# A pre-norm transformer block with ternary feed-forward weights on one core: the normalisation of attention in two halves, Q and K three slots ahead, row normalisation on VectorE, and Q and K columns of the first weight first

## The reference

```
h = layernorm(x)                          # rows of 512, no gain
qkv = h @ Wqkv                            # Wqkv: 512 x 1536, 16 heads of 32
a = softmax(causal(q @ k.T * 32**-0.5))   # a batch and a head: 512 x 512
x = x + (a @ v) @ Wo
y = layernorm(x)
w = clip(round(w / mean|w|), -1, 1) * mean|w|     # for w1, w3 (1365 x 512), w2 (512 x 1365)
x = x + (silu(y @ w1.T) * (y @ w3.T)) @ w2.T
```

## Time and profile before

| | |
|---|---|
| median of 3 runs | 706.42 us (706.09 to 708.06) |
| profiled execution | 708.65 us |
| its span, first to last instruction | 706.9 us |
| TensorE matmul busy | 596.1 us, 84% |
| VectorE busy | 368.9 us, 52% |
| GpSimd busy | 347.5 us, 49% |
| ScalarE busy | 254.2 us, 36% |
| mean granted TensorE clock | 0.939 |

### The profile page before, as it was taken

One profiled execution on the slowest core, in us unless ns is written; L12 is line 12 of the kernel. 1 busy time (PEld: TensorE's weight loads), 2 busy tenths in 40 slices (PEclk: granted clock), 3 DMA queues, 4 the chain that ended last, 5 costly groups with the idle time before them and its releaser, 6 DMA issues.

```text
span 706.9 us, 9375 instructions
## 1 busy us (share of the span) xinstructions
PE 596.1 (84%) x3392; PEld 278.4 (39%) x3392; DVE 368.9 (52%) x917; ACT 254.2 (36%) x428; POOL 347.5 (49%) x364
## 2 busy tenths in 40 slices
PE   1866767776699798999998879999998986899998
PEld 1323224333244344444444334444443432444443
DVE  7486646636554656462565656453646553353431
ACT  1563618526223244422223424322333363202330
POOL 6350569355438295625083784433472754652330
PEclk9989786978899989999999999999999997899999
DMA  9743223131401200222304000223020000100001
GB/s 339 230 139 116 76 75 121 45 100 46 135 1 56 80 1 1 75 77 74 120 2 134 1 1 23 85 88 128 24 65 11 2 1 1 60 31 30 1 1 59
DMA packets 35569, 46.87 MB, mean 66 GB/s; under 512 B 4634, under 2 KB 25114, under 8 KB 35524
## 3 DMA queue, kind: packets, MB, share of 16 engines
q1 hardware_dynamic: 35524, 46.28, 20.1%
HBM read 33.55 MB, written 12.58 MB: 65 GB/s over the span
## 4 chain that ended last, share of the span: by engine, by line
PE 50%; POOL 18%; DVE 14%; ACT 8%; issue 4%; DMA 3%; SPq 1%; DVEq 0%; POOLq 0%; ACTq 0%
PE work L971 29%; PE work L1133 9%; DVE o_sb L837 6%; POOL xn L525 4%; POOL early L563 4%; ACT early L660 4%; PE work L1081 4%; POOL early L566 3%; POOL early L554 3%; DVE masked L828 2%; PE score_bank L1042 2%; PE work L1095 2%; PE prob_bank L1064 2%; POOL early L569 2%; DMA late<-in_L_attn_Wqkv 2%
## 5 line engine op out<-in xcount | busy, mean ns | idle before, releaser
L971 PE MATMUL work<-late,w_ternary 128*128 128x512 f16 (+1 forms) x704 | 170.3, 393 | 5.2 <-DVE o_sb L842 3.0
L828 DVE CUSTOM_DVE_ANT_0 masked<-score_bank,mask 128x512 f16<-128x512 f32 (+3 forms) x256 | 111.7, 485 | 14.1 <-PE score_bank L1042 14.0
L660 ACT ACTIVATE early<-prob_bank,scalars 128x512 f32<-128x512 f32 x160 | 100.7, 686 | 39.1 <-PE prob_bank L1064 38.8
L971 PEld LDWEIGHTS work<-late,w_ternary 128*128 128x128 f16 (+1 forms) x704 | 71.5, 103 | 83.7 <-issue 10.7
L580 POOL TENSOR_TENSOR late<-late 128x512 f16<-128x512 f32 (+1 forms) x44 | 50.7, 1157 | 81.6 <-ACT late L680 81.6
L1064 PE MATMUL prob_bank<-q_stack,k_stack 98*128 98x512 f16 (+3 forms) x256 | 58.3, 328 | 29.1 <-ACT early L660 28.6
L837 DVE RECIPROCAL o_sb<-work 128x512 f32<-128x512 f32 x16 | 53.7, 3358 | 47.4 <-PE work L1095 47.4
L1133 PE MATMUL work<-w_ternary,late 128*128 128x512 f16 (+1 forms) x352 | 78.0, 379 | 0.0
L574 POOL TENSOR_TENSOR ot_lo<-o_sb,ot_hi 128x512 f16<-128x512 f32 x16 | 18.5, 1157 | 117.4 <-ACT ot_hi L665 117.4
L1042 PE MATMUL score_bank<-k_stack,q_stack 96*128 96x512 f16 (+3 forms) x256 | 55.4, 321 | 19.5 <-DVE row_max L828 15.7
L858 DVE SCALAR_TENSOR_TENSOR late<-late,work 128x512 f32<-128x512 f32 (+1 forms) x44 | 30.2, 687 | 78.9 <-ACT late L673 78.9
(11 more groups left out here) (114 smaller groups left out, 857.4 us busy)
## 6 DMA issues: line engine op xcount, KB each, us to landing
xn<-in_L_attn_x SPq DMA_DIRECT2D x16, 256.0 KB, 4.1
q_stack<-q_hi_spill SPq DMA_DIRECT2D x32, 128.0 KB, 2.5
k_stack<-k_hi_spill SPq DMA_DIRECT2D x32, 128.0 KB, 2.6
late<-in_L_attn_Wqkv SPq DMA_DIRECT2D x4, 768.0 KB, 8.7
x_res<-in_L_attn_x SPq DMA_DIRECT2D x12, 256.0 KB, 2.9
out_y<-x_res SPq DMA_DIRECT2D x12, 256.0 KB, 2.0
late<-in_L_ffn_w SPq DMA_DIRECT2D x4, 682.5 KB, 4.1
early<-in_L_ffn_w SPq DMA_DIRECT2D x3, 768.0 KB, 13.8
```

The lines of the kernel that those rows point to most:

```text
L660: act.activation(probs[:, u, :], prob_bank[u % 2][:], ACT.Exp, scale=scalar(exp_scale)).then_inc(prob_free, 1)
L828: dve.tensor_tensor_reduce(masked[:, k % 2, 0:n], score_bank[u % 2][:, off:off + n], mask[:, S - n:S], 1.0, LOWEST, ALU.add, ALU.max, row_ ...
L971: last = pe.matmul(bank, lhs, rhs, start=(n == 0), stop=(n == len(terms) - 1))
```

## The change

- `sums` no longer normalises. A new step `normalise` with two halves of 256 columns does it: the first behind the first `probs` piece, the second behind the scores that follow. Both work banks come free with the second half.
- A new step `ot` (ScalarE and GpSimd) stands ahead of piece 2 of `probs`.
- `q` and `k` of slot s+3 are made in slot s; their halves go to a place of their own in DRAM for each slot, and a step `stack` loads the stacks of s+2 at the head of slot s. The first four slots' Q and K are made before slot 0.
- `norm` moves from GpSimd to VectorE. The second norm writes to `yn`, a new buffer of two row blocks; `xn` holds x alone.
- The loads of Wqkv bring the columns of Q and K first (four loads of 512 KB) and V in one. Q and K, V, and Wo have maxima and scales of their own.
- wo's maximum and split move from the prelude to slot 0. The mean of w3 and w2 comes one step later, with all that follows it. x of batch 1 is normalised and turned in slot 0, of batch 2 normalised in slot 3 and turned in slot 4.
- The down products of batch b-2 are laid in slot 0 of batch b (before: in slot 3 of batch b-1, for batch b-2), the projections and both sets of transposes too; slots 1 to 3 hold 6, 8 and 8 of the up products.

```diff
 def preparation(m, start):
-    steps[start + PARTS] = [("weight_mean", m)]
+    steps[start + PARTS + 1] = [("weight_mean", m)]
...
-        a = start + PARTS + 1 + c // 2
+        a = start + PARTS + 2 + c // 2
...
 def slot(s, early, late):
-    front = [[("scores", s + 1, 0)], [("scores", s + 1, 1)]] if s + 1 < SLOTS else [[]]
-    o = spread(front, early)
-    if s:
-        o += [("values", s - 1), ("sums", s - 1)]
+    o = [("scores", s + 1, 0)] if s + 1 < SLOTS else []
+    o += sum((steps for _, steps in early), []) + ([("values", s - 1)] if s else [])
+    o += [("scores", s + 1, 1)] if s + 1 < SLOTS else []
+    o += [("sums", s - 1)] if s else []
     back = []
     for p in range(PIECES):
-        back.append([("probs", s, p)])
+        back.append([("ot", s - 1)] if s and p == 2 else [])
+        back[-1].append(("probs", s, p))
         if s + 1 < SLOTS and p + 2 < PIECES:
             back.append([("scores", s + 1, p + 2)])
+        if s and p == 0:
+            back = [[("probs", s, 0), ("normalise", s - 1, 0)] + (back[1] if s + 1 < SLOTS else []) + [("normalise", s - 1, 1)]]
...
+def residual_rows(b, i):
+    return (2.5, [("project", b, i), ("stats_y", b, i), ("norm_y", b, i)])
...
 def order():
...
+    o += [("top_part", c) for c in range(KC)] + [("xt", 0, 0), ("xt", 0, 1), ("top_turn", "qk"), ("xt", 0, 2)]
+    o += [("xt", 0, 3), ("top_spread", "qk"), ("x_load", 1)] + [("split", j) for j in range(4)] + [("top_v",), ("q", 0)]
+    o += [("weight_sum", w1, 0), ("k", 0), ("top_turn", "v"), ("stack", 0), ("q", 1), ("top_spread", "v")]
+    o += [("weight_sum", w1, 1), ("split", 8), ("k", 1), ("stack", 1), ("weight_sum", w1, 2)]
...
+    o += [("weight_ternary", w1, c) for c in range(6, 9)] + [("q", 3), ("max_row", 0)]
...
+    o += [("k", 3)] + [("weight_turn", w1, c) for c in range(8, HC)]
...
-        early, late = qk(s + 2) if g != GROUPS - 2 else [], []
+        early, late = [(0.0, [("stack", s + 2)])] if 0 < s < SLOTS - 2 else [], []
+        ahead = 0 < s < SLOTS - 3
+        if ahead:
+            early += [(2.5, [("q", s + 3)])]
         if b == 0:
             late = {p: prep.pop(PIECES * s + p, []) for p in range(PIECES)}
...
+            if ahead:
+                late[0].insert(0, ("k", s + 3))
+            if g == 0:
+                late[0] += [("stats_x", 1, 0), ("stats_x", 1, 1), ("wo_max",)]
+                late[1] += [("stats_x", 1, 2), ("stats_x", 1, 3), ("norm_x", 1, 0), ("norm_x", 1, 1)]
+                late[2] += [("norm_x", 1, 2), ("norm_x", 1, 3), ("top_turn", "wo"), ("xt", 1, 0)]
+                late[3] += [("top_spread", "wo"), ("xt", 1, 1), ("xt", 1, 2)]
+                late[4] += [("wo_split",), ("xt", 1, 3), ("x_load", 2)]
+            elif g == GROUPS - 1:
+                late[1] += [("res_load", 0, i) for i in range(ST)]
+                for i in range(ST):
+                    late[i] += [("stats_x", 2, i)]
+                    late[i + 1] += [("norm_x", 2, i)]
         elif g == 0:
...
+            late = [(4.7, [("down", b - 2, i), ("res_load", b - 1, i)]) for i in range(ST)] if b > 1 else []
+            late += v[:1] + [(1.0, steps) for _, steps in sorted(prep.items())]
+            late += v[1:3] + y[:2] + v[3:] + yt[:1] + y[2:3] + yt[1:2] + y[3:]
             prep = {}
+            if not last:
+                late += [(0.4, [("xt", b + 1, i)]) for i in range(ST)] + [(0.0, [("x_load", b + 2)])]
+            early_yt = yt[2:]
             ups = ffn_up(b - 1)
...
+            n = 8 if g > 1 else 6
+            late, ups = ups[:n], ups[n:]
+            if g == GROUPS - 1 and b + 2 < BATCHES:
+                late = merged(late, [(0.3, [(step, b + 2, i)]) for step in ("stats_x", "norm_x") for i in range(ST)])
+        if b and ahead:
+            late.insert(0, (2.5, [("k", s + 3)]))
...
+            def stack(s):
+                if s >= STACKS:
+                    sp.wait_ge(prob_full, NU * (s - STACKS + 1))
+                else:
+                    sp.wait_ge(unit_rows_set, s + 1)
+                for n, stacks in (("q", q_stack), ("k", k_stack)):
+                    for part_ in ("hi", "lo"):
+                        sp.wait_ge(spilled[n, part_], 16 * (s + 1))
+                        for j in [j for j, at in enumerate(STACK_ROWS[n]) if at == part_]:
+                            sp.dma_start(stacks[s % STACKS][j * HD:(j + 1) * HD, :, :],
+                                         spill[n, part_][s].rearrange("(h d) s -> d h s", h=HG)).then_inc(stacked[n][s % STACKS], 16)
...
+            def norm(n, b, src, dst, i):
+                dve.wait_ge(rstd_done[n], ST * b + i + 1)
+                dve.tensor_scalar(dst, src, mean_var[n][:, i, 0:1], rstd[n][:, i:i + 1],
+                                  ALU.subtract, ALU.mult).then_inc(norm_done[n], 1)
+
+            def norm_y(b, i):
+                if i > 1:
+                    full(dve, ("yt", b, i - 2))
+                elif b:
+                    full(dve, ("yt", b - 1, i + 2))
+                norm("y", b, residual(b, i), yn[:, i % 2, :], i)
...
+            def normalise(s, part_):
+                cols = slice(part_ * S // 2, (part_ + 1) * S // 2)
+                sums, values = ("sums", s), ("values", s)
+                if part_ == 0:
+                    full(dve, sums)
+                    full(dve, values)
+                    if s:
+                        dve.wait_ge(o_lo_done, s)
+                    dve.reciprocal(o_sb[:, cols], work[bank_of(sums)][:, cols]).then_inc(inverted, 1)
+                    dve.wait_ge(inverted, s + 1)
+                    dve.tensor_tensor(o_sb[:, cols], work[bank_of(values)][:, cols], o_sb[:, cols], ALU.mult)
+                else:
+                    dve.reciprocal(o_sb[:, cols], work[bank_of(sums)][:, cols]).then_inc(work_free[bank_of(sums)], 1)
+                    emptied(dve, sums)
+                    dve.tensor_tensor(o_sb[:, cols], work[bank_of(values)][:, cols], o_sb[:, cols],
+                                      ALU.mult).then_inc(work_free[bank_of(values)], 1)
```

More of the change, by code:

```diff
@@ L155, in order @@
     o = [("pad", w1)] + [("stats_x", 0, i) for i in range(ST)] + [("norm_x", 0, i) for i in range(ST)]
[L156 to L166, removed]
@@ new lines, in order @@
+    o += [("weight_sum", w1, 1), ("split", 8), ("k", 1), ("stack", 1), ("weight_sum", w1, 2)]
+    o += [("v", 0, 0), ("weight_sum", w1, 3), ("scores", 0, 0), ("split", 4), ("split", 5), ("v", 0, 1)]
+    o += [("weight_mean", w1), ("scores", 0, 1)] + [("weight_round", w1, c) for c in range(HC)]
+    o += [("q", 2), ("weight_ternary", w1, 0), ("scores", 0, 2), ("k", 2), ("stack", 2), ("split", 6), ("split", 7)]
+    o += [("weight_ternary", w1, 1), ("weight_ternary", w1, 2), ("pad", w3)]
+    o += [("weight_load", w3, j) for j in range(PARTS)] + [("scores", 0, 3), ("v", 0, 2)]
@@ L169, in order @@
+    o += [("weight_ternary", w1, c) for c in range(3, 6)] + [("weight_turn", w1, 0), ("weight_turn", w1, 1)]
+    o += [("scores", 0, 4), ("v", 0, 3)] + [("weight_turn", w1, c) for c in range(2, 5)]
+    o += [("weight_ternary", w1, c) for c in range(6, 9)] + [("q", 3), ("max_row", 0)]
+    o += [("weight_ternary", w1, c) for c in range(9, HC)] + [("weight_turn", w1, c) for c in range(5, 8)]
+    o += [("k", 3)] + [("weight_turn", w1, c) for c in range(8, HC)]
     prep = preparation(w3, 0)
@@ L291, in build @@
         k_stack = [sb(f"k_stack{i}", [P, HG, S], F16) for i in range(STACKS)]
-        spill = {key: nc.dram_tensor("_".join(key) + "_spill", [P, S], F16, kind="Internal").ap() for key in half}
+        spill = {key: nc.dram_tensor("_".join(key) + "_spill", [SLOTS, P, S], F16, kind="Internal").ap() for key in half}
         masked = sb("masked", [P, 2, S], F16)
@@ L361, in build @@
         res_loaded = [sem(f"res_loaded{i}") for i in range(ST)]
-        wqkv_loaded = [sem(f"wqkv_loaded{i}") for i in range(KC)]
+        qk_loaded = [sem(f"qk_loaded{i}") for i in range(KC)]
+        v_loaded = sem("v_loaded")
         wo_loaded = sem("wo_loaded")
@@ L496, in _ @@
                 elif step[0] in ("q", "k"):
-                    place(step)
+                    spill_halves(step)
+                elif step[0] == "stack":
+                    stack(step[1])
                 elif step[0] == "max_row":
@@ L606, in _ @@
                         add(step[1], step[2] - 3)
-                elif step[0] == "sums":
-                    values(step[1])
+                elif step[0] == "ot":
+                    ot(step[1])
                 elif step[0] == "lin":
@@ L830, in maxima @@
                                                  row_max[:, h, tile:tile + 1]).then_inc(score_free, 1)
-            def sums(step):
-                s, bank = step[1], bank_of(step)
-                full(dve, step)
-                if s:
-                    dve.wait_ge(o_lo_done, s)
-                dve.reciprocal(o_sb[:], work[bank][:]).then_inc(work_free[bank], 1)
-                emptied(dve, step)
-                before = ("values", s)
```

(9 more changed lines are left out.)

164 lines of the change are left out of this document (65 added, 99 removed).

## The result

| | before | after |
|---|---|---|
| median | 707.24 us | 687.85 us |
| ratio, 95% interval | | 0.971 (0.967 to 0.976) |
| span of the profiled execution | 706.9 us | 686.8 us |
| TensorE busy | 596.1 us | 587.7 us |
| TensorE idle | 110.8 us | 99.1 us |

It is 2.9% faster, 20 us in the span; I had forecast 55, and 687.85 lies just above the wide range of 630 to 686. The 20 us are 11.7 of idle time of TensorE and 8.4 of busy time. The work is the same but for three small matmuls, so I put the busy time down to the clock: it is 11.2 us less in slots 4 to 15, where the granted clock rose from 0.96 to 0.98, and 2.8 more ahead of them. No run separates it.

What follows compares the result with a forecast made beforehand. TensorE was taken to lead, with idle time and low clock to win outside full slots. Terms 19 + 10 + 10 + 6 + 4, plus 10 of clock, less 4, made 55 us: 652 us, range 640 to 665 (wide 630 to 686).

Steps and rivals of the forecast that it cites:

- 19 + 10 + 10 less 4: Gains from exponentials' wait (19), halved normalisation (10) and norm on VectorE (10), less 4 us for a new wait.
- Order of the fills: Products redistributed over each batch's slots: no work goes, so the sum is unchanged and only the rivals are affected.
- The first stretch: End of the prelude and slots 0 to 3, 64.1 to 184.8 us: about 30 us shorter.
- the mean comes one step later: Weight preparation: TensorE waits less for ScalarE's sums, gaining 6 us of 5.9 + 6.6; ends 0 and 12.
- a gain of 4: wo's maximum and split leave the prelude and the first product comes 1.5 us earlier: both 4 us, ends 0 and 6.
- The second stretch: Slots after slot 3, 184.8 to 613.7 us: about 23 us shorter.
- Exponentials, 19 us: Slot's start: with the ot copy moved, two thirds of the 28.6 us wait for exponentials goes; ends 9 and 28.
- Halves, part of the 10 us: Normalisation in two halves: scores of piece 2 wait less, gaining 10 of 21.5 us; ends 0 and 16.
- Norm on VectorE, 10 less 4: Rows normalised on VectorE relieve GpSimd, 10 us; new wait for the reciprocal root and added VectorE work cost 4.
- the slower rival: Each of 28 VectorE norms waits for GpSimd's select and additions, costing 87 us: result 734 us; chance 0.05.
- The clock, 10: TensorE's low clock up to 613.7 us: fewer idle times give back 10 us; ends 0 and 25.
- Light slots: Nine slots with g = 1 to 3, batches 1 to 3, stay chain-bound: 677 us; chance 0.28, shared with a missing term.

Runs made afterwards that it cites:

- e11: Kernel before with row normalisation on VectorE and the new slot (halves, ot ahead of piece 2), old order of fills but V ahead of projections: 700.44 us.
- e3: Changed kernel with row normalisation put back on GpSimd, where the constants now stand ahead of it: 715.41 us.
- e13: Changed kernel with w2's preparation two steps later, wo's maximum, scale and split in the prelude, x's statistics and norms of batches 2, 3 in long slots: 671.14 us.
- e5: Changed kernel with the whole preparation of w2 two steps later (step 11, not 9): 684.70 us.
- e4: Changed kernel with the output weight's maximum, scale and split back in the prelude: 685.54 us.
- e1: Changed kernel with both halves of the normalisation and the ot copy put back ahead of the first probability piece: 721.15 us.
- e2: Changed kernel with one reciprocal and product over 512 columns at the first half's place, ot staying at piece 2: 690.24 us.
- e8: Kernel before with only the row normalisation moved to VectorE, still through the shared buffer: 743.61 us.

## Why the prediction was wrong

Two steps failed. The first is the sum itself: 19 + 10 + 10 less 4 are waits of the kernel before, taken as time that comes back whatever else changes. In the kernel before, these parts together gave 7 us for the 35 (e11), singly they cost 36 and 6, and in the new order they give 59 (746 to 688, of which up to 6.7 belong to the constants of e3). The second is "Order of the fills. No work goes; the sum isn't changed by it": with the parts in, the order cost 14.6 us in the first stretch and gave 28.3 in the second. The worth of every removed wait hung on it.

**The first stretch** (forecast about 30 us shorter, measured 4.4 longer). The norm and the new slot alone, in the old order, shorten it by 10.2 us (e11). The new order lengthens it by 14.6 (189.2 against 174.6), and e13 gains 18.0 there by order alone. Its parts: 6.7 us for w2's sums in front of its loads (e5), 4.0 for the output weight in slot 0 (e4), and 7.0 for x's statistics and norms in slot 3, which takes 22.1 us in e13 and 29.1 in e5; together 17.7. The first is a wait that the change added and I priced as a gain: I took "the mean comes one step later" for 6 us, and the mean's own wait (5.9) did go, but the loads of w2 wait for w3's ternary chunks, which moved with the mean, while w2's sums stayed where they were. Exponentials stand behind them on ScalarE. I had named no queue behind that step. The second stood in the prediction as part of a gain of 4.

**The second stretch** (forecast about 23 us shorter, measured 24.6). The number is right by luck. I had it from the removed waits with the order at nothing; in the old order these parts cost 3.7 us there, and only with the new order do they gain.

**Exponentials, 19 us.** Their wait fell by 11.8. In the new order the place of ot is worth 33 us, all of it behind slot 3, and nothing in the first four slots, though half of the old wait (14.2 of 28.6 from 64 to 185 us) lay there. That slots of 23.5 and 28.2 us have no room for the 4.7 us of the earlier trace rows fits with e1, where the nine light slots take some 3.2 us more each; the reason is argued. In the old order the new slot costs 6 with GpSimd's norms and gains 43 with VectorE's, 16.1 of it in the first four slots. One number for this term was never to be had.

**Halves, part of the 10 us.** At most 2.4 in the new order (e2). The half reciprocal takes 1.75 us and the product 0.42, as estimated.

**Norm on VectorE, 10 less 4.** Worth 27.6 in the new order (some 21 without the constants), minus 36 in the old with the old slot, 13 with the new slot. The mechanism of the slower rival was right: e8 shows VectorE's wait for the root and TensorE's behind it. Either of the other parts takes it away: with the new order alone (e1) the waits for the root are 18.6 us and TensorE's for the maxima 7.8, with the new slot alone (e11) 38.1 and 14.2. The order stands x's statistics ahead of its norms and leaves y's back to back in the long slot only; that this is the reason is argued. The duration is 0.55 us with GpSimd idle and up to 2.03, mean 0.89 for x; I had 0.7. All 32 norms take 24.7 us, 7 more than 32 at 0.55, not the 58 more that the prediction gave as a bound.

**The clock, 10.** TensorE's busy time fell by 8.4 us. Near in size, but all in the second stretch: the clock of the first fell from 0.82 to 0.76, and the mean is 0.945 (0.939 before) where I had 0.96.

**The start, 1.5 us.** The maximum of all Q and K columns is on its way to TensorE at 15.34 us and was at 16.90, and the first product leaves at 20.81 and left at 22.37, 1.6 us earlier. The end of the prelude (68.6, with two more Q and K pairs than at 64.1) says no more on it.

**The rivals and signs.** Light slots did not stay chain-bound: TensorE is 97 to 100% busy in slots 5, 6 and 9 to 11, and 87% in slot 7, where x's rows stand. Only slots 13 to 15 are as that rival had them, 24.0 to 25.4 us with 20 to 21 busy. So the time fell where the prediction had put "light slots or a missing term", by missing terms. The signs for the forecast missed as well: 16.8 us of wait for the exponentials and not under 12, 11.5 for the maxima and not 8, 19.3 for the root and not under 15.

## What to carry to other kernels

Price the order, not the step: move a step, and list for each thing that waits on it (a load, a sum) whether that moved too, and what stands behind the waiter on its engine. Before adding terms, ask of each stretch whether the wait to be removed will still set its length in the new order; here the same edit was worth 16 us in the first four slots in one order and nothing in the other. Parts that relieve each other's engines can't be judged alone: each of the three costs time by itself, and together they gain. And when a part is taken back as an experiment, look whether its old place is free: in e3 the constants stood there.

## What the runs showed of the hardware

A VectorE norm that began 0.07 us behind a GpSimd addition of 1.81 us took 2.03 us, about the addition's rest and 0.3 more, against 0.55 at 210.07 with no addition beside it. GpSimd's side can suffer as well: the split of the output weight on VectorE and an addition on GpSimd that is 1.27 us in the earlier trace rows met (timeline of the changed kernel) and both grew, the split from the 2.35 us that it took in the kernel before:

```profile
93.39 3.40 DVE L816 SCALAR_TENSOR_TENSOR wo_lo<-late,scalars,wo_hi 128x2048 f16<-128x2048 f32 x1 [1.61 <-ACT wo_hi L628]
94.73 3.19 POOL L574 TENSOR_TENSOR early<-early 128x512 f32<-128x512 f32 x1
```

The Trainium skill ("SBUF — State Buffer", Who interferes with whom) says that a two-port VectorE operation and GpSimd exclude each other for a whole instruction, and that an operation with two SBUF inputs contends with GpSimd's reads. Both rows agree with it.
